# A fused chain of four conv and attention layers: conv units of slots 13 to 23 in three blocks of six, small gate products placed beside products of the same form, no products of ones ahead of the even part

## What is computed

```python
# L0: channel attention and a gate
att = softmax(max(E) - E), E = einsum('bcn,bdn->bcd', q, q)
out = einsum('bcd,bdn->bcn', att, q)
se = sigmoid(relu(mean([x, out]) @ w1.T + b1) @ w2.T + b2)      # z0
x = se * x + (1 - se) * out
# L1: reduce to 64 channels, depthwise 3x3, attention in the Fourier domain
xr = relu(bn(dwconv(reduce(x))))
g = sigmoid(relu(mean(xr) @ gate_w1.T + gb1) @ gate_w2.T + gb2)  # z1
y = post(concat(attended(fft2(xr)), ifft2(fft2(xr) * fft2(g * xr)))) + x
# L2: group norm, attention over pixels with 8 heads, projection, residual
x = x + proj(softmax(q k) v)
# L3: three 3x3 convs (q, k, v), attention over images, norm, relu, 3x3 conv
x = x + conv3x3(relu(norm(softmax(q k / sqrt(C)) v)), Wc)
```

## Time and profile before

| | us |
|---|---|
| median of 3 runs | 503.41 (501.46 to 505.49) |
| the profiled execution | 503.86 |
| its span in the trace | 502.1 |
| TensorE busy | 476.3 (95%) |
| VectorE busy | 343.5 (68%) |
| ScalarE busy | 253.6 (51%) |
| GpSimd busy | 126.1 (25%) |
| mean granted clock of TensorE | 0.976 |

### The profile page before, as it was taken

The page is one execution under the profiler, slowest core; times in us unless marked ns, Lnnn a source line. Parts: engine busy times, 40 slices in busy tenths (PEclk is TensorE's granted clock), DMA queues, the critical chain, the costliest instruction groups (busy, mean ns, idle before and its releaser), DMA issues.

```text
span 502.1 us, 10621 instructions
## 1 busy us (share of the span) xinstructions
PE 476.3 (95%) x3827; PEld 384.2 (77%) x3827; DVE 343.5 (68%) x890; ACT 253.6 (51%) x598; POOL 126.1 (25%) x154
## 2 busy tenths in 40 slices
PE   8999999899999999999999999999997999998996
PEld 7877775776687777768786877777675789898995
DVE  1448577967777786787777877876484442776895
ACT  4424756655656455555546464544623431294551
POOL 5122343474012112211210121120110011342662
PEclk9999999998999999999999999999995899997999
DMA  6000012020000000000000000000000000005112
GB/s 228 22 21 3 1 48 69 1 70 23 1 21 23 1 2 21 21 0 0 21 21 0 21 0 0 0 23 1 1 21 1 1 23 1 1 1 168 38 51 79
DMA packets 9487, 13.18 MB, mean 26 GB/s; under 512 B 496, under 2 KB 8816, under 8 KB 9328
## 3 DMA queue, kind: packets, MB, share of 16 engines
q1 hardware_dynamic: 9456, 12.76, 7.9%
HBM read 8.57 MB, written 4.19 MB: 25 GB/s over the span
## 4 chain that ended last, share of the span: by engine, by line
PE 73%; DVE 12%; ACT 6%; issue 4%; POOL 3%; DMA 1%; DVEq 0%; ACTq 0%; POOLq 0%
PE bank L1230 9%; PE bank L1232 8%; PE bank L1231 8%; PE bank L1432 5%; PE bank L1349 5%; PE bank L1381 4%; PE bank L1406 4%; PE bank L1237 4%; PE bank L1404 2%; PE bank L1460 2%; PE bank L1447 2%; PE bank L1254 1%; DVE nmax L1005 1%; ACT prob L749 1%; PE bank L1419 1%
## 5 line engine op out<-in xcount | busy, mean ns | idle before, releaser
L1230 PE MATMUL bank<-win,w_hi 128*128 128x256 f32 x384 | 117.2, 305 | 1.7 <-DVE win L1034 1.0
L1232 PE MATMUL bank<-win,w_lo 128*128 128x256 f32 x384 | 109.1, 284 | 0.0
L1231 PE MATMUL bank<-win,w_hi 128*128 128x256 f32 x384 | 108.9, 284 | 0.0
L749 ACT ACTIVATE prob<-bank 128x512 f32<-128x512 f32 x128 | 69.5, 596 | 65.9 <-PE bank L1404 65.2
L1005 DVE TENSOR_REDUCE nmax<-bank 128x2 f32<-128x512 f32 x128 | 84.9, 686 | 25.8 <-PE bank L1381 25.3
L1230 PEld LDWEIGHTS bank<-win,w_hi 128*128 128x128 f32 x384 | 73.2, 191 | 8.0 <-DVE win L1034 2.1
L1231 PEld LDWEIGHTS bank<-win,w_hi 128*128 128x128 f32 x384 | 73.5, 191 | 0.4
L1232 PEld LDWEIGHTS bank<-win,w_lo 128*128 128x128 f32 x384 | 73.3, 191 | 0.0
L534 POOL TENSOR_TENSOR first<-first 128x256 f32<-128x256 f32 x24 | 17.6, 735 | 151.2 <-ACT first L637 151.2
L1237 PE MATMUL bank<-ones_r 128*128 128x256 f32 x281 | 52.3, 324 | 1.1 <-DVE ones_r L854 1.1
L1406 PE MATMUL bank<-qk 32*128 32x256 f32 x256 | 41.2, 338 | 7.2 <-ACT prob L749 5.8
(11 more groups left out here) (243 smaller groups left out, 910.2 us busy)
## 6 DMA issues: line engine op xcount, KB each, us to landing
w_stage<-convs SPq DMA_DIRECT2D x4, 576.0 KB, 4.1
x_in<-x SPq DMA_DIRECT2D x8, 256.0 KB, 2.7
out<-x_pair SPq DMA_DIRECT2D x8, 256.0 KB, 2.2
q<-out SPq DMA_DIRECT2D x1, 2048.0 KB, 8.2
out<-v SPq DMA_DIRECT2D x8, 256.0 KB, 2.1
cst<-small SPq DMA_DIRECT2D x1, 1712.0 KB, 9.4
cst<-small SPq DMA_DIRECT2D x1, 253.5 KB, 3.0
```

Source lines behind the costliest of these rows:

```text
L749: act.activation(prob[:, x // 4 % 2, x % 4, :, :], bank[ST_BANK[x % 2]][:, :], ACT.Exp, scale=L2_SCALE).then_inc(st_exp, 1)
L1230: mm(dst, hi, x_hi, start=(row == 0), stop=False)
L1231: mm(dst, hi, x_lo, start=False, stop=False)
L1232: return mm(dst, lo, x_hi, start=False, stop=(row == KH - 1))
```

## The change

It has five parts. (1) The 18 units of slots 13 to 23, before in blocks of three in slots 13, 15, 17, 19 and 21 and one and two in slots 22 and 23, are in blocks of six in slots 13, 17 and 21. By `conv_events` the first copies go from slots 15 and 23 to 13 and 21, the sums from 16 and 24 to 14 and 22; the join of the first group stays at slot 20 by a new entry in `JOIN_SLOTS`. (2) z1 and z0 stand right behind the slot's scores. (3) hid0 goes to slot 12, patt to 13, and post_att on VectorE from 14 to 13. (4) The two products of ones ahead of even are gone, with a wait for `joined`. (5) The weight split of pair 1 goes from slot 17 to 15, its low part from 19 to 17.

```diff
 PE_SLOTS = {...
-            "hid0": 13, "filt": 12, "z0": 14, "patt": 14, "y1": 15, "gsum": 17, "red": 19}
+            "hid0": 12, "filt": 12, "z0": 14, "patt": 13, "y1": 15, "gsum": 17, "red": 19}
...
-DVE_SLOTS = {... "gate": 12, "post_att": 14,
+DVE_SLOTS = {... "gate": 12, "post_att": 13,
...
+PE_BESIDE = ("z1", "z0")
...
-CONV_NOW = (0, 0, 0, 0, 0, 0, 0, 0, 0, 0, 0, 0, 0, 3, 0, 3, 0, 3, 0, 3, 0, 3, 1, 2)
+CONV_NOW = (0, 0, 0, 0, 0, 0, 0, 0, 0, 0, 0, 0, 0, 6, 0, 0, 0, 6, 0, 0, 0, 6, 0, 0)
...
-JOIN_SLOTS = {1: SLOTS + 2, 2: SLOTS + 8}
+JOIN_SLOTS = {0: 20, 1: SLOTS + 2, 2: SLOTS + 8}
...
-MIX_SLOTS, SPLIT_SLOTS, WLOW_SLOTS = ((2, 13), (2, 10)), ((9, 16), (6, 17)), ((10, 19), (7, 19))
+MIX_SLOTS, SPLIT_SLOTS, WLOW_SLOTS = ((2, 13), (2, 10)), ((9, 16), (6, 15)), ((10, 19), (7, 17))
...
+                    for what, i in parts(PE_SLOTS, s, early, late):
+                        if what in PE_BESIDE:
+                            stage(what, i)
                     if s == 1:
                         project(j, "v")
...
                     for what, i in parts(PE_SLOTS, s, early, late):
-                        if what == "even" and left:
-                            pe.wait_ge(joined, 3 * cj)
-                            keep_busy(BUSY_EVEN, CONV)
-                        stage(what, i)
+                        if what not in PE_BESIDE:
+                            stage(what, i)
```

More of the change, by code:

```diff
@@ L65 @@
 PE_SLOTS = {"xt": 2, "hid1": 3, "z1": 4, "energy": 4, "xht": 5, "dft": 7, "att0t": 7, "o0": 8, "dot1": 9, "even": 11,
-            "hid0": 13, "filt": 12, "z0": 14, "patt": 14, "y1": 15, "gsum": 17, "red": 19}
+            "hid0": 12, "filt": 12, "z0": 14, "patt": 13, "y1": 15, "gsum": 17, "red": 19}
 ACT_SLOTS = {"xr": 0, "xt": 2, "hid1": 3, "z1": 4, "sum_x": 5, "att0": 6, "att0t": 7, "ab": 7, "o0": 11, "even": 11, "att1": 11,
              "hid0": 13, "filt": 13, "z0": 14, "red": 19}
-DVE_SLOTS = {"n2m": 1, "xh": 3, "xht": 5, "e_min": 5, "att0_inv": 7, "logit1": 9, "att1_n": 12, "gate": 12, "post_att": 14,
+DVE_SLOTS = {"n2m": 1, "xh": 3, "xht": 5, "e_min": 5, "att0_inv": 7, "logit1": 9, "att1_n": 12, "gate": 12, "post_att": 13,
              "se": 16, "x2": 16, "x1": 17, "gvar": 17, "xn": 19, "taps0": 20, "taps1": 21, "taps2": 22}
+PE_BESIDE = ("z1", "z0")
 POOL_SLOTS = {"rn": 1, "squares": 8, "diff0": 12, "grstd": 18}
@@ L92 @@
 EVENTS, EVENTS_LAST = conv_events(CONV_NOW, CONV_NEXT), conv_events(CONV_LAST, ())
-BUSY_AHEAD, BUSY_EVEN, BUSY_PAIR_1 = 14, 2, {s: 3 for s in range(13)}
+BUSY_AHEAD, BUSY_PAIR_1 = 14, {s: 3 for s in range(13)}
 BUSY_PAIR_0 = {1: 6, 2: 6, 3: 6, 4: 6, **{s: 3 for s in range(5, 16)}, 16: 6, 17: 6, 18: 6, 19: 6}
```

## The result

The changed kernel takes 518.96 us (median of 4 runs, 516.45 to 520.44) against 504.45 us before (4 runs, 501.46 to 506.42): ratio 1.0291, 95% interval 1.0247 to 1.0334. Forecast were 516 us, in a range of 505 to 523. The profiled execution has a span of 515.9 us, 13.8 more than before.

The account below looks back on a forecast made before the run. TensorE's queue was taken to set the pair (busy 45.05 of 46.00 us). Profiled 503.9 us + 6.4 for the pairs + 6.0 for clock falls = 516.3; with the median 0.45 below the profiled run, 516 us, range 505 to 523.

Parts of the forecast that it names:

- Cost of the units: Convolution units in blocks of six, 2.24 us each, instead of three: net 0.45 us saved a pair.
- Slot 15: y1 waits for z0's exponential, 2.05 us after scores_t(6), against 1.01 of TensorE work: new 1.04 us stop, pairs 1 to 5.
- Slot 19: heads_t waits for VectorE's normalise, about 1.48 us from result_t's start, without the block between: 1.06 us stop, pairs 1 to 7.
- z1 and ones: z1 beside 32-row products saves 0.2 us in seven pairs; removing the ones ahead of even saves 0, at most 0.34.
- Pair 1: Ordinary +1.45 us, less 2.6 for the removed result_t stop (1.1) and the clock fall behind it (1.5): -1.1.
- Pair 6: No z0 of a next pair, but the maxima wait for two row maxima, +0.37 us; with the rest +0.8.
- Pair 7: No y1: -0.5, stops of 1.4 and 1.06 us, less about 1.1 if half clock ends earlier: +0.9 us.
- The clock: Of twelve new stops of 1 us, four bring a clock fall at 1.5 us: +6.0 us, bounds 0 and 15.
- Rival 1: Both stops (slots 15 and 19) appear but the clock does not fall: 510 us, chance 0.24.
- Rival 2: The new stops are absorbed as stops in slots 8 to 12 shrink, +0.6 us a pair: 505 to 506, chance 0.10.
- Rival 3: Fewer blocks save entry and exit, and z0's exponential and the normalise come in time: faster, 494.5 us, chance 0.07.
- Rival 4: The clock falls in nearly every pair, twice in some: 525 us, chance 0.09.

Follow-up runs that it names:

- both repairs: Changed kernel with z0 in slot 13 on TensorE and ScalarE, and three units put back in slot 19: 505.72 us, ratio 1.0003 to the kernel before.
- the last-pair experiment: Kernel before with products of ones added in slots 8, 9 and 11 of the last pair (8, 10 and 7): 500.71 us, ratio 0.9941.

## Why the prediction was right, step by step

- **The sum.** 516 us were forecast, with a range of 505 to 523; 518.96 were measured. The mechanism is the one forecast: two stops for chains that the change left as long as they were, and falls of the clock beside them. An ordinary pair, forecast at +1.45 us, measured +1.4 (pairs 3 to 5). But that the total came within 3 us is in part luck: pair 1 (-1.1 forecast, +2.5 measured) and pair 6 (+0.8, +3.0) were worse than forecast even with 1.5 us for a fall added, and the last pair (+0.9, -0.4) was better.
- **Cost of the units.** A block of six at 2.3 us was right. The saving of form (0.45 us a pair, with z1's 0.2 together 0.65) was right in sum: the two stops less the saving, 1.18 + 0.81 - 0.65, come to 1.34.
- **Slot 15.** Forecast 1.04 us, measured 1.18: the chain took 2.15 us from scores_t(6) to y1 and not 2.05, and TensorE's part 0.97. That z0's place on ScalarE is the cause is shown by moving it to slot 13.
- **Slot 19.** Forecast 1.06, measured 0.81. The chain was right (1.47 us); result_t holds TensorE 0.66 us when nothing follows it at once, and I had taken 0.42. Three units put back remove it.
- **z1 and ones.** The ones are worth nothing, as forecast. z1's 0.2 us a pair does not show by itself: all small moves together give 0.05 us a pair with the old blocks, though between the kernel with the blocks alone (47.9) and the changed one (47.5) they give 0.4. The term was mis-sized where the blocks are small.
- **Pair 1.** Forecast -1.1, measured +2.5; this term failed, in three parts. The fall that the change takes away was priced at 1.5 us and is worth 0.6. The order alone, without a fall, takes 48.5 and 48.6 us (the kernels with ones in both stops and at y1 alone), so -0.4 and not -1.1. And a new fall of 6.8 us behind heads_t added 2.9. I looked for who shares ScalarE with the weight split, and not for what GpSimd's low part, moved two slots ahead with it, does to VectorE: result_t's stop is gone, but gsum stops 0.46 us in the changed kernel (1.50 with the old blocks).
- **Pair 6.** Forecast +0.8; without a fall it took 44.8 us (ones in both stops), +1.45, and the fall of 3.4 us in the changed kernel added 1.55. Not in the forecast were 0.24 us more at scores(12) and 0.30 more for ScalarE's h_c (0.47 us in place of 0.17).
- **Pair 7.** Forecast +0.9 on the guess that the half clock ends earlier, priced at 1.1 us; it and all behind it measured -0.4. The half clock of the last pair was 6.8 us in place of 13.6 here, but 17 us with ones in the stops of the pairs before, so that guess was met in this execution and is no property of the change that the runs show.
- **The clock.** Forecast four falls at 1.5 us. Measured in pairs 1 to 6: three, two of which lasted twice as long as the one I priced by, 3.1 us each. The sum (some 6 us against the 6.0 forecast; 5.2 in the medians with ones) was right, its parts were not. That the stop at heads_t is the one that loses the clock is shown for pair 6; in pairs 1 to 5 most falls begin there, but only in kernels in which y1 stops too. In this section the Trainium skill (TensorE: Matmul & The Clock Gate, "HAM oscillation — how this bites in real kernels") ties a fall to longer gaps without work; by it rival 1's 510 us would have come out, and the trace disagrees: the clock fell three times beside a stop of 0.81 us.
- **Rivals.** Rival 1 (no fall) is out by the three falls, and the ones in both stops show what they cost. Rival 2 (stops absorbed) is out: in slots 8 to 12 the stops are 0.53 and 0.59 us, not smaller. Rival 3's saving by form exists, some 0.65 us a pair, against 2.0 of stops. Rival 4 (a fall in nearly every pair) was not met: three of pairs 1 to 6 had one.

## What to carry to other kernels

Long work that can stand anywhere is worth most where it fills round trips through other engines: before taking a block out, work out the chain beside it (product, other engines' operations in their own order, next product) and compare it with what is left on TensorE. A stop can cost again in granted clock, so where no useful work is left to fill one, products that nobody reads may pay: 25 of them in the last pair brought the kernel before 0.6%, though the version with both repairs gained nothing that its runs show clearly. A fall is worth only what no stop behind it takes back: one of 3.4 us cost 0.6 us in one pair and 1.55 in another. A slot number in an order by hand says only what comes behind what, so an operation moved to a later slot starts as soon as its engine is free.

## What was not expected of the hardware

VectorE's operations on 128x2 and 128x4 numbers, 0.16 to 0.23 us alone, took 0.85 to 1.55 us while a GpSimd operation on 128x768 or 128x384 was under way (118.93 to 122.66 in one kernel, 124.68 to 128.4 in another). In pair 1 of the changed kernel it was the first operation on z0's exponential, which stands in VectorE's order ahead of the statistics for which gsum then stopped 0.46 us:

```profile
117.86 1.55 DVE L881 TENSOR_SCALAR z0p<-z 128x2 f32<-128x2 f32 x1
```

```profile
117.56 1.82 POOL L499 TENSOR_TENSOR w_lo<-v,w_hi 128x768 fp32r<-128x768 f32 x1 [3.00 <-ACT w_hi L611]
```

The end fits too: they ended within 0.05 us of the end of a GpSimd operation (119.41 here against 119.38; 120.77 against 120.76 with the old blocks; 126.52 against 126.50 with the low part in slot 22), however much of it was left when they began. The Trainium skill (SBUF — State Buffer, section "SBUF: two separate sides") tells of a port pair of VectorE and GpSimd that one holds for its whole instruction; these ends agree with that. The Trainium skill limits it there to VectorE operations on two SBUF inputs or in a mode with two ports; the operations of 1.51 and 1.55 us have one tensor each, and whether they ran in such a mode no trace here shows. Nor did every VectorE operation wait: the two of x2, which read PSUM, took 0.88 us at 119.55 beside GpSimd's of 119.35, as they did in the kernel before at 117.24 with GpSimd idle.

The clock, once at 1.2 GHz, stayed there for 3.4 us at times and for 6.8, 10 or 13.6 at others, with TensorE busy all of 6.50 and 6.80 us in two of these stretches. Single runs of one kernel differ by 1% here, and the mean granted clock goes with it: of the kernel before, beside the last-pair experiment, the fastest run (500.89 us) had 0.989 and the slowest (507.41 us) 0.973.
